# A four-stage graph network over 16 samples: the loop of the layers written out, and new instruction lists for all engines

## The reference

```python
h = relu(_layernorm(x)); x = x + L0(h, adj)   # 8 Euler steps: h += dt*(alpha/2*(A@h - h) + h@w_eff - h + x0)
h = relu(_layernorm(x)); x = x + L1(h, adj)   # dense graph attention, one head, softmax over 512 neighbours
h = relu(_layernorm(x)); x = x + L2(h)        # attention over 256 edges, 4 heads, segment softmax
h = relu(_layernorm(x)); x = x + L3(h, adj)   # Laplacian product, then a transformer layer:
#   scores = q @ k.T / sqrt(32), masked by adj; softmax; @ v; @ Wo; layer norm; gelu MLP; layer norm
```

## Time and profile before

| | us |
|---|---|
| median of 3 runs (1178.1 to 1180.65) | 1180.29 |
| the profiled execution's own time | 1176.97 |
| its span | 1175.1 |
| PE busy | 1097.5 (93%) |
| DVE busy | 852.1 (73%) |
| ACT busy | 768.5 (65%) |
| POOL busy | 340.1 (29%) |

### The profile page before, as it was taken

How to read it: one execution, slowest core, us unless ns; L and a number is a source line. 1 busy time by engine, 2 the same in 40 slices (tenths; PEclk the granted TensorE clock), 3 DMA queues, 4 the chain that set the end, 5 groups by cost and what they waited for, 6 DMA issues and landing times. The chain is left out here.

```text
span 1175.1 us, 22865 instructions
## 1 busy us (share of the span) xinstructions
PE 1097.5 (93%) x7105; PEld 873.4 (74%) x7105; DVE 852.1 (73%) x3073; ACT 768.5 (65%) x1640; POOL 340.1 (29%) x465
## 2 busy tenths in 40 slices
PE   7999999999999977999999999999999999999685
PEld 4679899899898856777777777777777777766454
DVE  7774444354364477898898898898898898887655
ACT  4334534432232246898898898898898988987762
POOL 3312104103061012234325325225234244243213
PEclk9999999999999988999999999999999999999887
DMA  3002020021400112424334334334243243243420
GB/s 92 18 11 63 12 79 19 19 81 41 126 10 18 46 47 80 122 66 110 102 89 107 99 98 107 88 104 111 71 116 99 82 122 86 79 113 85 113 64 27
DMA packets 132895, 88.86 MB, mean 76 GB/s; under 512 B 13664, under 2 KB 115424, under 8 KB 132832
## 3 DMA queue, kind: packets, MB, share of 16 engines
q1 hardware_dynamic: 132768, 88.07, 27.6%
q0 software_dynamic: 64, 0.00, 0.0%
HBM read 33.50 MB, written 20.97 MB: 46 GB/s over the span
## 5 line engine op out<-in xcount | busy, mean ns | idle before, releaser
L2453 DVE CUSTOM_DVE_ANT_0 att_Ts<-bank,mask_att 128x512 f32<-128x512 f32 x256 | 174.7, 683 | 64.1 <-PE bank L2608 62.0
L2355 ACT ACTIVATE att_Es<-att_Ts,att_small 128x512 f32<-128x512 f32 x256 | 185.3, 724 | 35.1 <-DVE att_small L2453 34.4
L2662 PE MATMUL bank<-ident,att_Es 128*128 128x128 f32 x1024 | 159.1, 279 | 16.9 <-ACT att_PTs L2364 12.4
L2364 ACT COPY att_PTs<-bank 128x512 f32<-128x512 f32 x248 | 144.0, 581 | 46.2 <-PE bank L2662 45.6
L2662 PEld LDWEIGHTS bank<-ident,att_Es 128*128 128x128 f32 x1024 | 121.8, 143 | 55.3 <-ACT att_PTs L2364 26.0
L2608 PE MATMUL bank<-K_parts,Q_parts 128*128 128x512 f32 x256 | 124.5, 496 | 4.7 <-DMA K_parts<-k_lo 3.2
L2149 POOL TENSOR_SCALAR n_rs<-n_mv 128x4 f32<-128x4 f32 x46 | 13.3, 290 | 309.2 <-DVE n_mv L2144 309.1
L1593 PE MATMUL bank<-G_hi,UT_parts 128*128 128x384 f32 x288 | 77.3, 338 | 1.8 <-DVE G_lo L1436 1.8
L2608 PEld LDWEIGHTS bank<-K_parts,Q_parts 128*128 128x128 f32 x256 | 48.0, 192 | 23.9 <-issue 16.8
L563 PE MATMUL bank<-gat_whs,gat_ETs 128*128 128x128 f32 x512 | 63.8, 280 | 2.0 <-PEq L149 2.0
L563 PEld LDWEIGHTS bank<-gat_whs,gat_ETs 128*128 128x128 f32 x512 | 61.9, 196 | 2.3 <-issue 2.2
(11 more groups left out here) (350 smaller groups left out, 2906.3 us busy)
## 6 DMA issues: line engine op xcount, KB each, us to landing
Q_parts<-q_hi SPq DMA_DIRECT2D x128, 64.0 KB, 2.0
Q_parts<-q_lo SPq DMA_DIRECT2D x128, 64.0 KB, 2.0
K_parts<-k_hi SPq DMA_DIRECT2D x128, 64.0 KB, 2.0
K_parts<-k_lo SPq DMA_DIRECT2D x128, 64.0 KB, 2.0
...
```

Of the source, the lines that this page charges most:

```text
L2355: nc.scalar.activation(att_E[:, j % RING_E, :], att_T[:, j % RING_T, :], ACT.Exp, scale=-1.0, bias=att_small[:, 0, j:j + 1], accum_out=att ...
L2364: nc.scalar.copy(att_PT[:, h, :, cols(q)], c2[:].rearrange("p (s q) -> p s q", q=P)).then_inc(sem("att_pt"), 1)
L2453: nc.vector.tensor_tensor_reduce(att_T[:, j % RING_T, :], [c0, c1][j % 2][:], k.mask_att[:, tile_of(n, j)[1], :], -QK_SCALE, HUGE, ALU.add ...
L2662: mm = nc.tensor.transpose(dst[:, cols(s)], att_E[:, i % RING_E, cols(s)], k.ident[:])
```

## The change

- `run` has no hardware loop any more: the ten iterations are written out by a Python loop, so that every sample number is a constant, and every wait is one on a constant.
- All lists are new: `ORDER`, `FILL_ORDER`, `DRAIN_ORDER`, for all five engines. The stage `att` begins one iteration earlier (`LAG`), and almost all of its steps have one "+" more, so most of it stands where it did; `att_score0` stands ahead of the end of the iteration before.
- On PE the scores run up to three tiles ahead of the turns (two before).
- Waits that others implied are now written: `att_score j` waits for the mask two tiles before for every j, `att_mask j` for the exponential three tiles before; `gat_exp0` and `gat_max0` wait for `gat_small`.

```diff
@@ gat_exp / gat_max @@
+            if t == 0:
+                ready(act, "gat_small", n, 4, 4)
...
+            if t == 0:
+                ready(dve, "gat_small", n, 1, 4)
@@ lags and lists (two lines of the new PE list; all others are replaced too) @@
-LAG = {s: i for i, s in enumerate(STAGES)}
+LAG = {"gat": 0, "edge": 1, "cheb": 2, "att": 2, "ffn": 4}
...
-        att_score0 att_score1 att_turn15+ att_rows+ att_pv0+ att_pv1+ att_score2 gat_turn att_turn0 att_score3 ffn_wo
+        att_score1+ cheb_v+ att_turn15++ att_rows++ att_pv0++ att_pv1++ att_score2+ att_score3+ att_turn0+ gat_turn
+        ffn_wo cheb_prop0 cheb_prop1 att_score4+ att_turn1+ att_score5+ cheb_g gat_wh ffn_turn att_turn2+ gat_s2
...
-FILL = 1 + max(LAG[STAGE_OF[step.rstrip("+")]] + step.count("+") for order in ORDER.values() for step in order)
+FILL = 6
@@ run @@
-            with fori(FILL, B) as i:
+            for i in range(FILL, B):
                 iteration(i)
@@ att_mask @@
-                if last(n):
-                    need(dve, sem("att_exp"), n * TILES + j + 1 - RING_T)
+                need(dve, sem("att_exp"), n * TILES + j + 1 - RING_T)
@@ att_score @@
-                if j in (2, 3) or last(n):
-                    need(pe, sem("att_T"), n * TILES + j - 1)
+                need(pe, sem("att_T"), n * TILES + j - 1)
```

More of the change, by code:

```diff
@@ L1867 @@
+        cheb_x1turn att_score9+ edge_gather0 edge_gather1 att_turn6+ att_score10+ att_score11+ edge_x att_turn7+
+        cheb_q edge_lcol gat_eturn0 att_turn8+ edge_lb0 gat_eturn1 att_score12+ edge_lb1 cheb_k gat_eturn2 att_turn9+
+        gat_eturn3 att_score13+ edge_v edge_den att_score14+ att_turn10+ gat_pv0 att_turn11+ edge_scatter att_score15+
+        att_turn12+ att_score0 edge_out att_turn13+ gat_pv1 att_turn14+
     """.split(),
     "DVE": """
-        cheb_stats cheb_aggr gat_x2a+ att_rv+ gat_x2b+ gat_stats att_mask0 gat_aggr edge_stats att_mask1 edge_aggr
@@ L1870 @@
[L1870 to L1874, removed]
+        edge_max1+ edge_max2+ edge_max3+ edge_le+ att_mask12++ edge_rden+ att_mask13++ cheb_klow+ edge_attn+ edge_u+
@@ L1875 @@
+        cheb_qlow edge_max0
     """.split(),
     "ACT": """
[L1877 to L1880, removed]
@@ L1897 @@
[L1897 to L1901, removed]
@@ L1902 @@
[L1902 to L1916, removed]
@@ new lines @@
+        att_score12:0 edge_lb1:2 att_score13:0 cheb_q:1 att_turn9:0 att_score14:0 gat_eturn1:3 gat_eturn2:3
+        att_turn10:0 edge_v:2 cheb_k:1 att_turn11:0 edge_den:2 gat_eturn3:3 cheb_v:1 att_score15:0 att_turn12:0
+        edge_scatter:2 gat_pv0:3 att_turn13:0 att_score0:1 edge_out:2 att_turn14:0 att_score1:1 att_score2:1 gat_pv1:3
+        att_turn15:0 att_rows:0 att_pv0:0 att_pv1:0 att_score3:1 att_turn0:1 att_score4:1 gat_turn:4 ffn_wo:0
+        att_score5:1 gat_wh:4 cheb_prop0:2 att_turn1:1 cheb_prop1:2 att_score6:1 gat_s2:4 att_turn2:1 ffn_turn:0
@@ new lines @@
+        att_score7:1 cheb_g:2 ffn_up0:0 ffn_up1:0 att_score8:1 att_turn3:1 ffn_down0:0 ffn_down1:0 att_score9:1
+        att_turn4:1 edge_gather0:3 edge_gather1:3 att_turn5:1 gat_eturn0:4 edge_x:3 att_turn6:1 att_score10:1
+        edge_lcol:3 att_turn7:1 gat_eturn1:4 att_score11:1 edge_lb0:3 cheb_x1turn:2 edge_lb1:3 att_score12:1
+        att_turn8:1 gat_eturn2:4 cheb_q:2 att_turn9:1 gat_eturn3:4 edge_v:3 edge_den:3 cheb_k:2 att_score13:1
+        att_turn10:1 edge_scatter:3 att_score14:1 att_turn11:1 att_score15:1 edge_out:3 att_turn12:1 cheb_v:2
@@ L1918 @@
+        edge_lcol:4 gat_eturn0:5 gat_eturn1:5 edge_lb0:4 edge_lb1:4 att_turn8:2 gat_eturn2:5 cheb_k:3 att_score12:2
+        att_score13:2 att_turn9:2 edge_v:4 gat_eturn3:5 edge_den:4 att_turn10:2 att_score14:2 gat_pv0:5 att_turn11:2
+        edge_scatter:4 att_score15:2 att_turn12:2 att_score0:3 edge_out:4 att_turn13:2 gat_pv1:5 att_turn14:2
     """.split(),
     "DVE": """
-        cheb_stats:0 gat_rinv:1 cheb_aggr:0 cheb_lo:0 gat_x2a:1 gat_x2b:1 gat_stats:2 gat_aggr:2 edge_stats:1
-        edge_aggr:1 gat_apply:2 cheb_y:0 n1_stats:0 n1_aggr:0 gat_scores0:2 n1_apply:0 gat_scores1:2 gat_scores2:2
@@ L1922 @@
[L1922 to L1931, removed]
```

277 lines of the change are left out of this document (151 added, 126 removed).

## The result

| | before | after |
|---|---|---|
| median, us (4 runs each) | 1179.19 (1175.63 to 1180.65) | 1218.74 (1215.52 to 1221.89) |
| profiled execution, us | 1176.97 | 1221.28 |
| its span, us | 1175.1 | 1219.3 |

The changed kernel is slower: ratio 1.035, 95% interval 1.032 to 1.038. I had forecast 1159.5 and put the chance of slower at 0.13.

The account below looks back on a forecast made before the run. PE was taken as the bound, DVE and ACT close behind. Twelve periods (-16.8), fill (-2) and drain (-2) sum to -20.8 us, from the median 1180.29 to 1159.5; whole range 1148 to 1178.

Parts of the forecast that it names:

- The period of 43.9: Steady loop: changed waits sum to -1.4 us a period, giving 43.9; twelve periods give -16.8.
- The terms on PE's own list: Steady period on PE: -0.4 - 0.6 - 0.1 - 0.35 - 0.26 + 0.2 + 0.15 = -1.4 us.
- `ffn_down0` waits 0.55: MLP: PE's wait before `ffn_down` falls from 1.14 to some 0.55 us, counted as -0.6.
- the turn behind the gelus: MLP, second half of `ffn_down`: a turn there found 0.25 us late, as one was at this place before.
- no wait before `edge_lb`, the last `gat_eturn` and `edge_out`: Edge and gat on PE: waits of 0.4, 0.35 and 0.26 us go, hidden by other steps.
- `att_score0` 0.2 behind the keys: Steady period: keys land 9.2 us after `cheb_k` starts, so PE waits 0.2; bounds nothing and 1.0.
- `edge_lcol` and `edge_den`: Edge: the first up to 0.4 us late, netted with `edge_lb` to -0.1; the second waits for ACT's exponential, +0.15.
- Fill: -2 (bounds 0 and -5): Before the loop: PE's 3.46 us wait for `gat_turn:3` shrinks, `gat_stats:3` and `gat_aggr:3` standing far ahead on DVE.
- Drain: -2 (-6 to +4): After the loop: same kind of gain in samples 13 and 14, with ever fewer stages to fill with.
- Waits on constants: 0, at most 0.6: Loop written out: some 0.15 us off masks DVE waits for, counted as nothing; upper bound four masks, 0.6 a period.
- "Slower": Rival, 1185 us, chance 0.13: keys reach `att_score0` late, a wait of 2.4, each period 0.8 longer than now.
- "Half": Rival, 1170 us, chance 0.22: DVE or ACT becomes the bound, leaving -0.6 a period, -7, with -3 for the ends.

Follow-up runs that it names:

- e10: Changed kernel with, in POOL's loop list, `ffn_x3b` moved behind `n3_rstd` and `edge_lo` behind `ffn_b2`: 1201.75 us, ratio 1.022 to the kernel before.
- e4: Kernel before with only its loop over samples 6 to 15 written out, same instruction lists: 1174.75 us, ratio 0.9988 to the kernel before.
- e9: Changed kernel with only `ffn_x3b` moved in POOL's loop list, to behind `n3_rstd`: 1203.05 us, ratio 1.022 to the kernel before.
- e7: Changed kernel with SP's lists of fill and drain reordered, loop untouched: 1176.10 us, ratio 0.9992 to the kernel before.
- e11: Changed kernel with SP's fill and drain lists, POOL's drain list, and `ffn_x3b` and `edge_lo` in POOL's loop reordered: 1155.81 us, ratio 0.981 to the kernel before.

## Why the prediction was wrong

The forecast was -20.8; the profiles are +44.2 apart. The 65.0 between lie in the fill (14.7), the first period (10.3), the eleven others (16.7), the drain (18.3), and the first part's clock (5.0).

*The period of 43.9.* The terms on PE's own list came about nearly as worked out. In the period from 788.49: `ffn_down0` waits 0.55 from start to start (forecast 0.55); the turn behind the gelus 0.28 late (0.25); no wait before `edge_lb`, the last `gat_eturn` and `edge_out`; `att_score0` 0.2 behind the keys (0.2). `edge_lcol` and `edge_den` are under 0.1 late, where I had 0.1 to 0.4 and 0.15. One reading was too large: at `edge_out` I took 0.26 for a wait, but a score ahead of transposes takes 0.33 with no wait (828.17 to 828.50), not 0.23, so only 0.16 was to be won. What failed is a step that I had not written as one: "a group of four transposes" at `ffn_turn` stood in my sum with no new wait, because I took the durations of DVE's instructions from the trace of before and only their order from the new list. The order put two of POOL's 128x512 instructions beside `n2_apply`, which grew by 1.95, and `ffn_turn` lost 1.43: just the -1.4 of my sum. Without that collision the period is 43.77 (e10), 0.1 from the forecast. That it is so close is in part luck: 0.18 of it is writing out (e4), which stood in my sum at nothing, and made up for terms that were too large. So "43.9" was about right of PE, and wrong of the kernel.

A rule that I should have weighed is of the Trainium skill, "SBUF — State Buffer", section "Who interferes with whom": VectorE with two inputs in SBUF and GpSimd reading SBUF share a port, and whichever starts second waits until the other's instruction ends. The runs agree: `n2_apply` has two inputs in SBUF and ended 0.15 after POOL's; the masks, whose first input is in PSUM, took 0.68 beside POOL's instructions as elsewhere. GpSimd's 128x4 instructions, the 1.04 us power among them, read SBUF too, and held nothing: 66 of the two-input instructions of 128x128 lay beside them in the ten periods and took 0.34 to 0.35. The rule as it stands does not say so, and here the measurement decides. By that rule the new lists give, as an estimate from the 1.29 us that `edge_lo` takes in the trace of before, a wait of at most 1.3 for each 128x512 instruction that `n2_apply` runs into. e9 and e10 took 1.0 and 0.9 a period off `n2_apply`, and 1.05 and 0.5 off the period.

*Fill: -2 (bounds 0 and -5).* It was +12.7, and the first period +8.9 more. I followed DVE and POOL up to `gat_apply:3` ("stand far ahead") and took the load before them as given. The failed step is that one: `gat_x2a:2` is ahead of it on DVE, in order, and needs a DMA whose place in SP's list I had not counted. 33 issues of 0.63 stood between, and the waits in front of them. The earlier trace rows had the price of an issue, 0.59 and a little more; counted, it gives 20.8 of the 38.3 us, and the keys and queries for which SP stands still would have to be followed for the rest. With SP mended the fill is -4.1 to -6.6 (e7, e11), about my lower bound or past it.

*Drain: -2 (-6 to +4).* It was +16.3, outside the bounds. Here the failed assumption is that a drain's list differs from the loop's in density only. Its order on SP was another (`load_xr:12` behind three heads), and it held POOL, ACT, DVE and PE in turn. With SP's and POOL's lists mended (e11) the drain is 137.0 from sample 12's values product to the end, against 142.2 before and 158.5 after: -5.2, near the lower bound. But most of this is not the lists: e4, with the drain lists of before, took 138.5, with less of its last 56 us at the lower clock (mean 0.84 for 0.79). Against that the mended lists win 1.5.

*Waits on constants: 0, at most 0.6.* -0.18 a period, by e4. The written-out period of the fill that I judged by (535.00 to 580.52) told nothing: it takes 45.5 in e4 too, and those behind it there 45.06, so something else rules it. What, was not looked into.

*The rivals.* "Slower" named the keys; they were not it, 0.2 late as in the forecast. "Half" named DVE as the next bound; the place was right (PE does wait for DVE), but by longer instructions, not by too many. (Its terms, added up, leave -0.45 a period and not -0.6, so 1172.) None of the rivals looked at SP's list outside the steady state, where the 39.6 us came from, or at what POOL runs beside DVE. My chances put 0.80 on one period's sum and let 232 us of fill and drain ride on two estimates of 2.

What stays open: why the first part, with the same code, differs by up to 7.4 us between executions; the profiles show it as time at the lower clock level, not its cause. And that two inputs in SBUF is the condition was not tested by changing an operand; it is read from which instructions grew and which did not. Why GpSimd's 128x4 instructions hold nothing is not shown either.
